# One PSUM bank per image for the attention scores, narrower query/key weights, and a new order of work in a four-image transformer block

## What is computed

```
x = x + attention(ln_c(x))          # q, k of 16 channels, softmax over 256 pixels, v of 64 channels
t = tokens(x)                       # 4 x 256 tokens of 64 channels
t = t + experts(ln_t(t))            # second layer norm, top 2 of 8 experts, each 64 -> 256 -> gelu -> 64
```

## Time and profile before

| what | value |
|---|---|
| median of three executions | 65.83 us |
| lowest, highest | 65.71, 65.84 us |
| the profiled execution's own time | 65.81 us |
| its span in the profile | 64.0 us |
| PE busy | 57.9 us (90%) |
| ACT busy | 33.3 us (52%) |
| DVE busy | 32.4 us (51%) |
| POOL busy | 24.6 us (38%) |

### The profile page before, as it was taken

One profiled execution on the slowest core, in us unless ns is written; L12 is line 12 of the kernel. 1 busy time (PEld: TensorE's weight loads), 2 busy tenths in 40 slices (PEclk: granted clock), 3 DMA queues, 4 the chain that ended last, 5 costly groups with the idle time before them and its releaser, 6 DMA issues.

```text
span 64.0 us, 1191 instructions
## 1 busy us (share of the span) xinstructions
PE 57.9 (90%) x356; PEld 33.2 (52%) x356; DVE 32.4 (51%) x152; ACT 33.3 (52%) x78; POOL 24.6 (38%) x48
## 2 busy tenths in 40 slices
PE   1987799799799999999999999999999999999940
PEld 0314356398445677955266285283643718722630
DVE  2367779458997799674007992040402204024730
ACT  5301337823349997709937729539195592930000
POOL 5165690000660895515059916143060003403500
PEclk9999999999999999999999999999999999999999
DMA  0442469720000000000056720006681000011011
GB/s 0 97 96 43 160 112 400 243 88 0 5 0 0 5 10 0 0 0 9 1 157 200 209 105 0 10 9 177 200 219 51 0 0 0 0 41 48 3 41 41
DMA packets 4270, 4.45 MB, mean 70 GB/s; under 512 B 2196, under 2 KB 2840, under 8 KB 4264
## 3 DMA queue, kind: packets, MB, share of 16 engines
q1 hardware_dynamic: 3944, 4.34, 22.9%
q10 hardware_dynamic: 320, 0.03, 0.5%
HBM read 4.08 MB, written 0.29 MB: 68 GB/s over the span
## 4 chain that ended last, share of the span: by engine, by line
PE 67%; DVE 18%; DMA 4%; SPq 3%; issue 3%; ACT 2%
PE banks L856 25%; PE banks L883 23%; PE banks L813 5%; DMA X<-in_x_dram 4%; DVE nmax L509 3%; PE banks L866 3%; PE banks L798 3%; DVE KS L503 2%; DVE X L495 2%; PE banks L835 2%; SPq L245 2%; PE banks L900 2%; ACT PR L378 2%; DVE T L527 2%; DVE X L559 1%
## 5 line engine op out<-in xcount | busy, mean ns | idle before, releaser
L414 ACT ACTIVATE H<-banks,PF 128x512 f32<-128x512 f32 x32 | 19.8, 683 | 9.3 <-PE banks L856 9.3
L856 PE MATMUL banks<-XE,W1F 64*128 64x256 f32 x128 | 16.8, 394 | 0.0
L883 PE MATMUL banks<-H,W2F 128*64 128x512 f32 x64 | 15.3, 603 | 0.0
L856 PEld LDWEIGHTS banks<-XE,W1F 64*128 64x128 f32 x128 | 11.4, 186 | 5.7 <-issue 4.4
L321 POOL TENSOR_TENSOR acc<-acc,gated 128x512 f32<-128x512 f32 (+1 forms) x6 | 6.5, 1088 | 16.5 <-DVE gated L639 16.5
L639 DVE SCALAR_TENSOR_TENSOR gated<-banks,B2T,GS 128x512 f32<-128x512 f32 (+1 forms) x7 | 4.6, 672 | 11.3 <-PE banks L883 11.3
L307 POOL TENSOR_SCALAR XE<-XF,PF,LB 128x256 f32<-128x256 f32 x15 | 8.2, 562 | 5.3 <-ACT XF L395 5.3
L754 PE MATMUL banks<-zeros 128*128 128x512 f16 x23 | 7.6, 450 | 1.3 <-POOL zeros L324 1.3
L291 POOL TENSOR_TENSOR rs<-base,half 128x4 f32<-128x4 f32 x4 | 4.0, 1012 | 9.9 <-DVE base L552 9.9
L883 PEld LDWEIGHTS banks<-H,W2F 128*64 128x64 f32 x64 | 4.0, 136 | 6.9 <-issue 6.7
L813 PEld LDWEIGHTS banks<-V,PTS 128*128 128x128 f32 x32 | 3.9, 191 | 0.9 <-issue 0.9
(11 more groups left out here) (78 smaller groups left out, 64.8 us busy)
## 6 DMA issues: line engine op xcount, KB each, us to landing
GS<-gates_kept SPq DMA_DIRECT2D x16, 128.0 KB, 3.0
W1F<-in_w_dram SPq DMA_DIRECT2D x1, 768.0 KB, 4.5
W2F<-in_w_dram SPq DMA_DIRECT2D x1, 512.0 KB, 5.0
W1F<-in_w_dram SPq DMA_DIRECT2D x1, 256.0 KB, 3.3
out_dram<-res SPq DMA_DIRECT2D x4, 64.0 KB, 1.6
X<-in_x_dram SPq DMA_DIRECT2D x2, 64.0 KB, 2.0
X<-in_x_dram SPq DMA_DIRECT2D x1, 128.0 KB, 2.5
WQK<-in_attn_w_dram ACTq DMA_DIRECT2D x2, 16.0 KB, 2.1
```

The lines of the kernel that those rows point to most:

```text
L414: nc.scalar.activation(H[:, r, :].rearrange("p (t n) -> p t n", t=PT), ps_z[g // J % 2][:, :, PIX * j:PIX * j + PIX], ACT.Gelu, bias=PF[:, ...
L856: nc.tensor.matmul(ps_z[q % 2][:, k, PIX * j:PIX * j + PIX], W1F[rows, e, j, :], XE[h][rows, e, :], start=True, stop=True).then_inc(z_read ...
L883: mm = nc.tensor.matmul(ps_y[s % 2][C * k:C * k + C, :], W2F[:, u, :], H[:, (2 * J * s + J * k + j) % RING, :], start=(j == 0), stop=(j == ...
```

## The change

- Scores and transposed probabilities of image i lie in one bank, 4 + i, so that each image has its own (before: two images shared two pairs). The waits of `scores(2)` and `scores(3)` for the copies of images 0 and 1 are gone.
- q and k come from one weight of 64 columns per tile: q on the output partitions 0 to 31, k on 32 to 63. Both tiles of q lie on the same 32 partitions, and both score matmuls of an image use the same 32 rows.
- The copy of an image's probabilities is one instruction of 128x512 on one engine: DVE for image 0, ACT for images 1 to 3 (before: one half on each, for every image).
- The third DMA of x is now the third on SP's queue. The weights of q and k come by two DMAs on ACT's queue; their biases by one instead of two.
- `ps_x1` of image 1 and `ps_O` of image 1 have banks of their own (3 and 0).
- Fillers between the calls of the attention: 10 instead of 15. The first eight stay.
- The lists of calls of all five engines are in another order.

```diff
-        ps_x1 = banks[:, 0, 0:P]
-        ps_q = [banks[0:C, 1 + k, 0:P] for k in range(2)]
-        ps_k = [banks[C:P, 1 + k, 0:PIX] for k in range(2)]
+        ps_x1 = [banks[:, 3 if i == 1 else 0, 0:P] for i in range(IMAGES)]
+        ps_q = [banks[0:DB, 1 + k, 0:PIX] for k in range(2)]
+        ps_k = [banks[DB:C, 1 + k, 0:PIX] for k in range(2)]
-        ps_S = [banks[:, 4 + PT * k:4 + PT * k + PT, 0:PIX] for k in range(2)]
+        ps_S = [banks[:, 4 + i, :].rearrange("p (t n) -> p t n", t=PT) for i in range(IMAGES)]
...
-        WQK = sb("WQK", [P, PT, P])
+        WQK = sb("WQK", [P, PT, C])
...
             sp.dma_start(X[:, PT:TILES, :], x[:, PT:TILES, :]).then_inc(x_in[1], 16)
+            sp.dma_start(X[:, TILES:2 * TILES, :], x[:, TILES:2 * TILES, :]).then_inc(x_in[2], 16)
             sp.wait_ge(w_clear, 1)
-            for k in range(PT):
-                rows = slice(C * k, C * k + C)
-                sp.dma_start(WQK[rows, 0, DB * k:DB * k + DB], attn_w[rows, A_WQ:A_WQ + DB]).then_inc(wqk_in, 16)
-            sp.dma_start(X[:, TILES:2 * TILES, :], x[:, TILES:2 * TILES, :]).then_inc(x_in[2], 16)
...
             first_pow(0)
-            first_pow(1)
             pool.wait_ge(ident_ready, 1)
...
             last.then_inc(iota_ready, 1)
+            first_pow(1)
             add_bias(0)
...
-                if i >= IMG:
-                    pe.wait_ge(PT_even, i - IMG + 1)
-                    pe.wait_ge(PT_odd, i - IMG + 1)
                 for t in range(PT):
-                    rows = slice(DB * t, DB * t + DB)
-                    nc.tensor.matmul(ps_S[i % 2][:, t, :], QS[i // IMG][rows, i % IMG, :],
-                                     KS[i // IMG][rows, n:n + PT, :].rearrange("p t n -> p (t n)"),
-                                     start=True, stop=True).then_inc(S_ps, 1)
+                    last = nc.tensor.matmul(ps_S[i][:, t, :], QS[i // IMG][:, i % IMG, P * t:P * t + P],
+                                            KS[i // IMG][:, i % IMG, :], start=True, stop=True)
+                last.then_inc(S_ps, 1)
```

More of the change, by code:

```diff
@@ L93, in build_block @@
         BV = sb("BV", [P, C])
-        BQK = sb("BQK", [P, 2])
+        BQK = sb("BQK", [C, 2])
         PF = sb("PF", [P, F_END])
@@ L194, in build_block @@
         PT_ps = sem("PT_ps")
-        PT_even = sem("PT_even")
-        PT_odd = sem("PT_odd")
+        PT_kept = [sem(f"PT_kept{i}") for i in range(IMAGES)]
         O_ps = sem("O_ps")
@@ L336, in _ @@
             last.then_inc(iota_ready, 1)
+            first_pow(1)
             add_bias(0)
+            add_bias(1)
             first_pow(2)
             first_pow(3)
-            add_bias(1)
             second_pow(0)
             second_pow(1)
-            for e in range(1, 8):
+            for e in range(1, 5):
                 stretch(0, e)
             second_pow(2)
+            stretch(0, 5)
             second_pow(3)
-            for e in range(0, 8):
+            stretch(0, 6)
+            stretch(0, 7)
+            for e in range(0, 5):
                 stretch(1, e)
@@ L351, in _ @@
             add_up(3)
+            for e in range(5, 8):
+                stretch(1, e)
             add_up(5)
@@ L737, in _ @@
-            route(1, 10)
-            weigh(0)
             weigh(1)
@@ L928, in _ @@
             turn_x1(0)
[L929 removed]
+            keep_warm(7, 3)
+            turn_x1(1)
             queries_keys(0)
[L931 to L932 removed]
+            keep_warm(7, 1)
+            queries_keys(1)
+            keep_warm(7, 1)
             scores(0)
[L934 removed]
             values(0)
[L936 removed]
+            turn_x1(2)
             scores(1)
             values(1)
[L939 to L943 removed]
             queries_keys(2)
             turn_x1(3)
+            turn_probs(0)
+            scores(2)
+            queries_keys(3)
+            attend(0)
+            turn_probs(1)
+            scores(3)
+            values(2)
             attend(1)
[L947 to L948 removed]
+            turn_probs(2)
             turn_b2()
[L950 removed]
+            values(3)
+            turn_probs(3)
+            attend(2)
+            keep_warm(4, 1)
             turn_x2(0)
[L952 to L955 removed]
+            keep_warm(4, 3)
             turn_x2(1)
[L957 to L958 removed]
+            attend(3)
+            layer1(0)
+            layer1(1)
             logits(0)
[L960 to L965 removed]
+            keep_warm(4, 1)
             layer1(2)
[L967 removed]
             layer1(3)
             turn_x2(2)
[L970 removed]
+            layer1(4)
+            layer1(5)
             turn_x2(3)
[L972 to L975 removed]
+            turn_gates(0)
             layer1(6)
             layer1(7)
[L978 to L979 removed]
+            logits(1)
+            layer2(0)
+            layer2(1)
             layer1(8)
             layer1(9)
+            layer2(2)
             layer2(3)
@@ L984, in _ @@
             layer1(11)
-            layer2(4)
+            turn_gates(1)
+            fold_sum()
             layer1(12)
             layer1(13)
-            layer2(5)
+            layer2(4)
             layer1(14)
             layer1(15)
-            fold_sum()
+            layer2(5)
             layer2(6)
```

217 lines of the change are left out of this document (90 added, 127 removed).

## The result

| kernel | executions | median | ratio to before, 95% interval |
|---|---|---|---|
| before | 22 | 65.80 us | |
| the change | 22 | 66.32 us | **1.0053** [1.0037, 1.007] |

The change makes the kernel slower by a little, some 0.35 us, where 0.7 us less was forecast.

What follows compares the result with a forecast made beforehand. PE was taken as the bound, working or waiting from 5.2 to 59.5 us. Fillers -1.1, scores +1.7, boundaries +0.15 and -0.2, waits -1.2 sum to -0.65, say -0.7: 65.1 us, range 64.1 to 66.1.

Steps and rivals of the forecast that it cites:

- POOL, first half of the step: At the start, first_pow(1) ends at 5.7 instead of 5.2; norm and semaphores bring image 1's transpose to 6.4.
- The 0.4 for the late power: PE's wait before image 1's transpose, wanted at 6.0 but ready at 6.4 because first_pow(1) stands later on POOL.
- Gates of the second half: Moving turn_gates(1) before layer1(12) still lets the gates' DMAs land in time for layer2(6) and layer2(7): cost 0.
- The slack of the broadcasts: Second half's gates land at 52.6 and 53.9, leaving slack of 1.4 and 0.5 before layer2(6) and layer2(7).
- Waits, -1.2: PE's waits fall from 3.1 to 1.9: the attention's nearly vanish, new ones come where the experts begin.
- Scores, +1.7: Score matmuls sharing 32 rows no longer pair: a group's pace goes from 0.63 to 1.06, +0.43 for each of four images.
- the 109 ns: Issue-gap rule for 256-column matmuls: four take 0.44, so the scores' term is 0; rival at 63.4, chance 0.03.
- the slower rival: Score matmuls cannot hide their weight loads, records 0.3 apart: +1.0 on the sum, so +0.3, 66.1; chance 0.18.
- Boundaries, +0.15 and -0.2: PE's changes of matmul shape go from 35 to 36 at 0.15 each; shorter 64-column weight loads give back 0.2.
- Fillers, -1.1: Five fewer fillers on PE in the attention, each 0.22 and all on the path.
- DMAs, 0: The third x DMA lands at 4.15, so first_stats(2) fits before first_norm(0) can run at 4.47: no cost.

Runs made afterwards that it cites:

- bias_late: The changed kernel with POOL's two bias additions moved behind the powers of images 2 and 3: ratio to before 0.996, median 65.72 us.
- pow_first: The changed kernel with POOL's power for image 1 back right behind that of image 0, bias additions unmoved: ratio to before 0.9906, median 65.38 us.
- gates_early: pow_bias with DVE's last two steps of the second half's gates moved ahead of weigh(3): ratio to before 0.9864.
- combo: The changed kernel with both POOL moves, the gates' last steps ahead of weigh(3) and 128-column q and k weights: ratio to before 0.9837, 64.7 us.
- fillers_back: pow_bias with five fillers put back between PE's groups, 15 as before: ratio to before 1.0062, profiled 66.47 us.
- pow_bias: The changed kernel with both POOL moves, those of bias_late and pow_first: ratio to before 0.9942, median 65.50 us.
- before_serial: The kernel before with both score matmuls of an image on the same 32 rows, nothing else: ratio to before 1.0084, +0.6 us.

## Why the prediction was wrong

The forecast was 65.1 from a sum of -0.65; measured was +0.35 (the profiled execution +0.31). The step that failed is the one on POOL: it priced the norm of image 1 as if it ran alone. A second one, on the gates, left out the same thing. By the forecast's steps:

- **POOL, first half of the step: wrong, the largest miss.** "Norm and semaphores bring it to 6.4" priced `first_norm(1)` at the 0.54 it takes when it runs alone. The step had counted what stands ahead of `first_pow(1)` and not what the change put right behind it, two bias additions that start in the same moment as the norm. Norm 1.47, transpose at 7.14: **+0.74** over the forecast, and the profiled execution of bias_late gives 0.71 back. The 0.4 for the late power was nearly right (0.3 by bias_late and pow_first).
- **Gates of the second half: wrong in what it left out.** The step looked at DMAs alone. The addition ahead of them stands behind `weigh(3)`, which also releases POOL's `add_up(3)`; it takes 1.20 instead of 0.19 and PE waits: **+0.39**. The slack of the broadcasts was right in its effect only. They come later than forecast, and the first `weigh` of the second half does wait for them, some 0.8 (its `layer2` is over at 52.4). It ends at 54.04, though, 2.1 ahead of `layer2(6)`, which needs it, so that PE loses nothing:

```profile
53.29 0.75 DVE L634 SCALAR_TENSOR_TENSOR acc<-banks,B2T,GS 128x512 f32<-128x512 f32 x1 [4.13 <-DMA GS<-gates_kept]
```

- **Waits, -1.2: right but for these two.** In the attention they vanished as laid out (14.32 busy of 14.36), and those of the GELUs came: the second and third pairs of `layer1` have paces of 2.20 (26.44 to 28.64) and 2.22 against 1.93 without a wait. Counted by starts and paces as in the forecast, the changed kernel waits 2.8: 1.1 for image 1's transpose, 0.4 for the second `turn_x2`, 0.8 for the GELUs and 0.5 for the gates' turn. Against the 3.1 of before that is -0.3.

```profile
26.44 2.27 PE L848 MATMUL banks<-XE,W1F 64*128 64x256 f32 x16
28.64 0.33 PE L818 MATMUL banks<-ident,X 128*128 128x128 f32 x1
29.08 2.29 PE L848 MATMUL banks<-XE,W1F 64*128 64x256 f32 x16
31.30 0.33 PE L818 MATMUL banks<-ident,X 128*128 128x128 f32 x1
```

- **Scores, +1.7: right.** Pace 1.06, 1.05, 1.03, 1.06 in the changed kernel, spacing 0.21 to 0.22 behind the first gap. In the order of before it would have cost 0.6 only, since PE waited there; in the change's own order, with next to no wait around them, the rows leave the full sum. So the 109 ns that the prediction took from the Trainium skill (TensorE: Matmul & The Clock Gate, Back-to-back issue gap) do not hold for these float32 records, and the slower rival, though it had the sign, named a mechanism that isn't there: the groups never reached the 1.23 from which it decides. Its price was mis-summed besides: a spacing of 0.3 adds 0.08 to the 0.217 of a record, not 0.18, so 1.3 for 16 records and not 2.9.
- **Boundaries, +0.15 and -0.2: right as PE's work.** The narrow weights were given seven boundaries at 0.15 less 0.2, 0.85 in all; the rows of gates_early and combo have 0.8. What leaving them out brings in time is less, 0.2 to 0.5.
- **Fillers, -1.1: right in kind, 0.2 too much.** 0.8 to 0.9 by fillers_back.
- **DMAs, 0: right.** `first_norm(0)` starts at 4.38, the third x transfer makes nothing late.

With the fillers at -0.9 and the waits at -0.3 the forecast's sum becomes -0.9 + 1.7 + 0.15 - 0.2 - 0.3 = +0.45, against +0.31 in the profiled execution: 0.1 us is not assigned.

The forecast's marks were 22.7 for the first `layer1` and 58.9 for the end of the last `layer2`; the changed kernel has 23.74 and 59.6. bias_late, which takes away the stretch and nothing else, has 23.03 and 58.9, and pow_bias 22.75 and 58.6. That 58.9 is met with the wait of 0.39 for the gates still in it, and 22.75 with slower fillers and without the wait for the power, is some luck.

That the first stretch, with `add_bias(0)` and `(1)`, was the cause is shown by bias_late and pow_first in two different ways; the part of `add_up(3)` in the second is read from the rows and from gates_early, and no kernel without that overlap was tried. A version that keeps the two query tiles of an image side by side and still gives each image its own bank wasn't tried.

## What to carry to other kernels

When a change moves a GpSimd tensor operation, look up what VectorE does at its new time, not only who waits for its result: a short VectorE instruction from SBUF to SBUF on the path can take the length of the GpSimd instruction beside it. A reordering that removes the waits makes PE's work worth nearly its full price; pair matmuls over different rows, and take out changes of shape, only after that. And price a moved step by its neighbours at both ends, on all engines, before counting its slack.

## What the runs showed of the hardware

- A DVE instruction on SBUF beside a POOL one: 1.47 instead of 0.51 to 0.61 for two of 64 elements, and 1.20 instead of 0.19 for one of 32. The end of the stretched instruction lies 0.04 or 0.05 behind that of POOL's in both places. Statistics, aggregates and a read from PSUM kept their lengths.
- float32 matmuls of 256 columns in one group of 32 rows start a record every 0.21 to 0.22 us (0.32 from the first to the second); two groups of 32 rows side by side do twice as much in the same 1.06.
- The trace of before had such a stretch too, off the path. The comparison of 32 elements (`hot`, two instructions) took 0.55 (at 23.83) and 0.54 beside POOL's work on the tokens (L307) and takes 0.28 in the changed kernel with POOL idle. That was there to be read before the forecast (the first two rows are of before):

```profile
32.76 4.37 POOL L307 TENSOR_SCALAR XE<-XF,PF,LB 128x256 f32<-128x256 f32 x8 [3.15 <-ACT XF L395]
...
36.15 0.54 DVE L602 TENSOR_TENSOR hot<-iota,topf 128x32 f32<-128x32 f32 x2
```

```profile
39.01 0.28 DVE L597 TENSOR_TENSOR hot<-iota,topf 128x32 f32<-128x32 f32 x2
```

- The last three fillers before image 1's transpose take 0.83 from start to next start in pow_bias (5.37 to 6.20) and 1.28 in gates_early (5.33 to 6.61), kernels that are alike up to there, with the clock granted in full in both profiles. 1.28 is 0.43 for each, twice the 0.22 of the 2.4 GHz level. So fillers can run at the pace of the 1.2 GHz level where the record of the granted clock reads full. How many do differs between executions: in eight profiles of kernels whose PE list is alike up to there (pow_first, pow_bias and all below but before_serial) image 1's transpose starts anywhere from 5.96 to 6.71. In a kernel without a wait behind these fillers that alone can move the time by up to 0.7 us, which is why small differences above were read from rows; in the changed kernel, whose transpose waits for DVE, it starts at 7.14 and, in another profile of it with fast fillers, at 7.09.

```profile
5.33 1.49 PE L747 MATMUL banks<-zeros 128*128 128x512 f16 x3
6.61 0.41 PE L754 MATMUL banks<-ident,X 128*128 128x128 f32 x1
```

```profile
5.37 0.99 PE L747 MATMUL banks<-zeros 128*128 128x512 f16 x3
6.20 0.27 PE L754 MATMUL banks<-ident,X 128*128 128x128 f32 x1
```
